# A recurrent block with a mixture of experts on one core: rows, halves of weights and the second layer's last tile in another order

## The reference, cut to what matters

```python
# x: (4, 256, 256) = 1024 tokens of 256 features
h = layernorm(x) * (1 + ca) + sa                    # sa .. gb: from silu(c) @ wmod, per batch
xn = rmsnorm(h, norm1_w)
left = gelu(xn @ left_W + left_b)
u = causal_depthwise_conv(xn @ right_W + right_b, conv_w, conv_b)     # 4 taps
right = rg_lru(u, ga_W, ga_b, gx_W, gx_b, a_param)  # two gates, then a scan over the tokens
x1 = left * right @ out_W + out_b + h
x1n = rmsnorm(x1, norm2_w)
mlp = gelu(x1n @ up1_W + up1_b) * (x1n @ up2_W + up2_b) @ down_W + down_b
x = x + ga * (mlp + x1)                             # "x2" in the kernel
h = layernorm(x) * (1 + cb) + sb
cw = top-2 of softmax(h @ gate_w), normalised       # 8 experts
moe = sum_e cw[:, e] * (gelu(h @ w1[e] + b1[e]) @ w2[e] + b2[e])
x = x + gb * (moe + h)
```

## Time and profile before

| what | value |
|---|---|
| median of 3 runs | 294.07 us (293.27 to 294.33) |
| the profiled execution's own time | 293.69 us |
| its span | 291.9 us |
| PE busy | 265.9 us (91%) |
| DVE busy | 200.3 us (69%) |
| ACT busy | 174.2 us (60%) |
| POOL busy | 128.9 us (44%) |

### The profile page before, as it was taken

One profiled execution on the slowest core, in us unless ns is written; L12 is line 12 of the kernel. 1 busy time (PEld: TensorE's weight loads), 2 busy tenths in 40 slices (PEclk: granted clock), 3 DMA queues, 4 the chain that ended last, 5 costly groups with the idle time before them and its releaser, 6 DMA issues.

```text
span 291.9 us, 4510 instructions
## 1 busy us (share of the span) xinstructions
PE 265.9 (91%) x1594; PEld 222.6 (76%) x1594; DVE 200.3 (69%) x459; ACT 174.2 (60%) x295; POOL 128.9 (44%) x104
## 2 busy tenths in 40 slices
PE   7997499999999999988999588999999999999970
PEld 2745246457788788866689588999999999999970
DVE  3659778937957777779877069685867676786520
ACT  4348449596089346960789139766859393939100
POOL 7009300000051312368075528738483839476651
PEclk9979599999999999999799869999999999999997
DMA  6990000000003757316145964929395766627233
GB/s 193 381 299 1 2 1 0 0 0 2 0 2 103 268 161 165 69 57 212 41 140 172 289 195 97 342 53 325 103 295 141 241 196 190 189 33 203 23 38 37
DMA packets 32838, 38.40 MB, mean 132 GB/s; under 512 B 7964, under 2 KB 28444, under 8 KB 32796
## 3 DMA queue, kind: packets, MB, share of 16 engines
q1 hardware_dynamic: 27184, 30.56, 33.4%
q0 software_dynamic: 4928, 7.44, 11.3%
q10 hardware_dynamic: 700, 0.07, 0.2%
HBM read 32.10 MB, written 8.90 MB: 140 GB/s over the span
## 4 chain that ended last, share of the span: by engine, by line
PE 50%; DVE 19%; DMA 9%; SPq 8%; issue 5%; ACT 4%; POOL 2%; POOLq 1%; DVEq 0%; ACTq 0%
PE bank L1007 15%; PE bank L1050 12%; PE bank L691 9%; SPq L505 5%; DVE u L1576 5%; PE bank L1044 3%; DMA x_rows<-blank 2%; PE bank L1043 2%; PE bank L891 2%; DMA gb_rows<-gb_table,meta 2%; DVE w_lo L1815 2%; DVE w_lo L1810 2%; SPq L509 1%; DMA x_tok<-in_L_attn_x 1%; PE bank L635 1%
## 5 line engine op out<-in xcount | busy, mean ns | idle before, releaser
L2109 POOL DMA_INDIRECT out_x<-y_tok,meta x24 | 53.3, 2219 | 38.2 <-DVE y_tok L1938 25.9
L1050 PE MATMUL bank<-w_hi,own 128*128 128x256 f32 x256 | 48.2, 283 | 0.0
L1920 DVE TENSOR_TENSOR own<-own_raw,own 128x256 fp32r<-128x256 f32 x64 | 27.2, 425 | 21.5 <-issue 13.2
L1007 PE MATMUL bank<-xe_hi,w_hi 128*128 128x320 f32 x128 | 39.9, 312 | 1.1 <-DVE xe_lo L1916 1.1
L1050 PEld LDWEIGHTS bank<-w_hi,own 128*128 128x128 f32 x256 | 40.9, 191 | 0.0
L1376 ACT ACTIVATE own_raw<-bank,b1c 128x320 f32<-128x320 f32 x64 | 33.5, 534 | 10.8 <-PE bank L1007 10.5
L1007 PE MATMUL bank<-xe_lo,w_hi 128*128 128x320 f32 x128 | 39.6, 309 | 0.0
L1007 PE MATMUL bank<-xe_hi,w_lo 128*128 128x320 f32 x128 | 39.6, 309 | 0.0
L1050 PE MATMUL bank<-w_lo,own 128*128 128x256 f32 x128 | 36.2, 283 | 0.0
L1382 ACT ACTIVATE own<-own_raw 128x320 fp32r<-128x320 f32 x64 | 29.8, 482 | 0.0
L2099 POOL DMA_INDIRECT gb_rows<-gb_table,meta x24 | 24.5, 1020 | 11.5 <-issue 6.7
(11 more groups left out here) (248 smaller groups left out, 636.5 us busy)
## 6 DMA issues: line engine op xcount, KB each, us to landing
e_raw<-in_L_ffn_w SPq DMA_DIRECT2D x16, 1024.0 KB
x_rows<-in_L_attn_x SPq DMA_DIRECT2D x1, 2560.0 KB
xe_tok<-x_rows SPq DMA_DIRECT2D x7, 256.0 KB
raw_m<-in_L_attn_up_W SPq DMA_DIRECT2D x2, 768.0 KB, 9.9
x_tok<-in_L_attn_x SPq DMA_DIRECT2D x2, 512.0 KB, 5.3
out_x<-x_tok SPq DMA_DIRECT2D x1, 1024.0 KB, 5.3
xe_tok<-x_rows SPq DMA_DIRECT2D x7, 128.0 KB
wmod<-in_L_wmod SPq DMA_DIRECT2D x1, 768.0 KB, 12.2
```

Of the source, the lines that this page charges most:

```text
L1007: ins = nc.tensor.matmul(bank[b][:, 0:CAP], l, r, start=(c == 0 and t == 0), stop=(c == KD - 1 and t == 2))
L1050: ins = nc.tensor.matmul(bank[b][0:n, 0:D], l, r, start=False, stop=(c == KE - 1 and t == 2))
L1920: nc.vector.tensor_tensor(own_lo[e % 2][:, f, :], own_raw[:, f % 4, 0:whole], own_hi[e % 2][:, f, 0:whole].bitcast(F32), ALU.subtract)
L2109: nc.gpsimd.indirect_dma_start(out_rows, bass.IndirectOffsetOnAxis(ap=ids[0:n, e, k, E:E + 1], axis=0), y_tok[e % 2][0:n, k, :], None, com ...
```

## The change

- **POOL** makes `wm_lo` as soon as its high halves are there; the split of the second bias comes after that and after the convolution (`conv_done`).
- **DVE, before the experts:** `rest(0)` goes from behind `v_of(KF + 5)`; two of the four picks of half 0 stand there, the other two behind the last `v_lo`. `w2_lo_of(0)` goes from behind `pick(1)` to behind `w1_lo_of(0)`, inside the MLP's last product. `rest(1)` goes too.
- **DVE, experts 0 and 1:** `rest(0)`, `rest(1)`, `rest(2)`, then `x_lo(1)` ahead of `keep_y(0, 0)`; `keep_y(0, 2)` and `w2_lo_of(1)` behind expert 1's low halves.
- **PE:** one gather ahead of `x2_and_logits(1, 1)`; the last tile of `second_layer(0)` behind `first_layer(1)`. The two banks of expert 0's gathers are exchanged.
- **ACT:** `w1_hi_of(2)` ahead of `x_hi(1)`, `keep_low(0)` behind `own_blocks(1)`.
- **SP:** the load of expert 2's first weights ahead of the wait for the `slot_a` scatters and `load_x(0)`.

```diff
-    take_at(("x0", 0), 3, 0)
-    take_at(("x0", 1), 1, 0)
+    take_at(("x0", 0), 1, 0)
+    take_at(("x0", 1), 3, 0)
...
                 load_w2(1)
+                sp.wait_ge(w1_lo_done, 2)
+                load_w1(2)
                 for t in range(TT):
                     sp.wait_ge(a_scattered[t], 16)
                 load_x(0)
-                sp.wait_ge(w1_lo_done, 2)
-                load_w1(2)
...
             down(1, [1], lambda: x2_and_logits(1, 0))
+            begin(("x0", 0))
+            gather(0, 0, 0)
             x2_and_logits(1, 1)
-            begin(("x0", 0))
-            for j in range(TH):
+            for j in range(1, TH):
                 gather(0, 0, j)
...
                 turn_of(1)
+                first_layer(1, EARLY, lambda: turn_of(2))
                 second_layer(0, [ST - 1])
-                first_layer(1, EARLY, lambda: turn_of(2))
...
                 w2_hi_of(1)
+                w1_hi_of(2)
                 x_hi(1)
+                own_blocks(1, lambda: x_hi(2))
                 act.wait_ge(rest_done, TT // 2)
                 keep_low(0)
-                w1_hi_of(2)
-                own_blocks(1, lambda: x_hi(2))
...
             v_of(KF + 5)
-            rest(0)
+            pick(0, range(TH // 2))
...
             nc.vector.tensor_tensor(v_lo[:, KF - 1, hs[1]], v_tile[(NH * KF - 1) % 4], v_hi[:, KF - 1, hs[1]].bitcast(F32), ALU.subtract).then_inc(v_lo_done, 1)
+            pick(0, range(TH // 2, TH))
             x2_of(1, [0])
             w1_lo_of(0)
-            pick(0)
-            rest(1)
+            w2_lo_of(0)
             x2_of(1, [1])
...
             pick(1)
-            w2_lo_of(0)
...
                     own_lo_of(0, f)
+                rest(0)
+                rest(1)
                 rest(2)
+                x_lo(1)
                 keep_y(0, 0)
                 rest(3)
                 keep_y(0, 1)
-                x_lo(1)
-                keep_y(0, 2)
-                w2_lo_of(1)
                 for f in range(KE):
...
                     own_lo_of(1, f)
+                keep_y(0, 2)
+                w2_lo_of(1)
...
+            for n in range(2):
+                pool.wait_ge(wm_hi_done, n + 1)
+                lo(wm_lo[:, n], raw_m[:, n], wm_hi[:, n], wm_lo_done)
+            pool.wait_ge(conv_done, NH * KH)
             pool.wait_ge(ffn_in, 16 * 4)
             pool.wait_ge(blank_done, 2)
...
             pool.wait_ge(b2_ready, 1)
-            for n in range(2):
-                pool.wait_ge(wm_hi_done, n + 1)
-                lo(wm_lo[:, n], raw_m[:, n], wm_hi[:, n], wm_lo_done)
-            pool.wait_ge(conv_done, NH * KH)
```

More of the change, by code:

```diff
@@ L1816, in w2_lo_of, with pick @@
                                         ALU.subtract).then_inc(w2_lo_done, 1)
-            def pick(hf):
+            def pick(hf, js=range(TH)):
                 if hf == 0:
@@ L1822, in pick @@
                     dve.wait_ge(gathered, 1)
-                for j in range(TH):
+                for j in js:
                     t = hf * TH + j
@@ L1979, in _ @@
                 nc.vector.memset(cwT[0:64, :], 0.0).then_inc(cw_cleared, 1)
-                rest(2)
-                rest(3)
+                for i in range(TT // 2):
+                    rest(i)
                 for i in range(TT // 2):
```

## The result

| | before | after |
|---|---|---|
| median, same chip, in turn | 294.20 us (293.27 to 294.83) | 282.79 us (281.83 to 283.80) |
| ratio, 95% interval | 1 | 0.9615 [0.957, 0.966] |
| profiled execution, its span | 293.69, 291.9 us | 283.80, 282.0 us |
| measured again, with the first experiments | 294.94 us | 283.04 us, 0.9565 [0.9491, 0.9638] |

The kernel is faster by 11.4 us (11.9 the second time); 280.4 was forecast, 13.3 less. The profiled execution, the slowest of its four, gained 9.9. Medians here are of all executions, and ratios leave out those over 1.5% above their kernel's fastest: one of `b_turn` (290.3 us, the profiled one) and two of `d_order` (289.17 us, and 339.78 us at a granted clock of 0.741).

The account below looks back on a forecast made before the run. PE, busy 91% of the span, was taken as the bound, each wait costing idle time and a lower clock. Gains of 5.0, 1.9 and 6.4 us sum to 13.3 off 293.69: 280.4 us, range 278 to 286.5.

Parts of the forecast that it names:

- POOL's order: First part, convolution of half 0 freed from POOL's subtraction: gates 3.8 plus clock 1.6 minus bias 0.4, 5.0 us gained.
- Gates: Behind the convolution of half 0: PE starts the gates at 29.05 instead of 32.89 us, 3.8 us gained.
- clock: First gate product on PE: without the long idle it takes 1.8 instead of 3.43 us, 1.6 us gained.
- bias: Recurrence of half 0 on DVE: POOL's bias split now meets it, delaying the out product, 0.4 us lost.
- The rival with 0.20: POOL's second subtraction gets in before the convolution's sixth operation; first part only 1.2 us, 284.2 us; chance 0.20.
- Around the last product: MLP's last product: picks of half 1, last gathers and expert 0 come 1.9 us earlier, bounds 0.7 and 2.9.
- The 0.89 us at `hT`: DVE's idle time at `hT`: transposes done in time with one gather less and the clock up, 0.9 us gained.
- the 1.3 us of the forecast for the scatters: Scatters ahead of expert 0: with `w2_lo` out of their way, the last one gains 1.3 us beyond the 1.9.
- Experts 0 to 2: Expert 0's full tiles to expert 2's start: waits and low clock 7.7, less 0.9 and 0.4, 6.4 us gained.
- the tokens 3.2 us earlier: they are there when PE arrives: Expert 1's tokens, asked for behind the weights: 3.2 us earlier, so PE's 2.9 us wait goes.
- expert 1's halves: PE's new wait from `turn_of(1)` to expert 1's first `x_lo`, through ACT and DVE: 0.9 us lost.
- The rival with 0.13: `gb_rows` land as late as before, past the harmless 165.7 us; last part 4.1, total 282.7 us; chance 0.13.

Follow-up runs that it names:

- b_turn: Changed kernel with expert 2's first weights (1 MB) asked for late and expert 1's transposes between expert 0's two full tiles; 287.20 us, ratio 0.9741.
- d_order: Changed kernel with ACT rounding the second up weights directly behind the first; profiled execution 287.7 us, others 283.82, 289.17 and 339.78 us.
- a_pool: Kernel before with POOL's reordering alone; 289.22 us, ratio 0.9805.
- a_trans: Kernel before with only the changes of PE, ACT, DVE and SP around experts 0 and 1; 293.51 us, ratio 0.9954.
- after_again: The changed kernel measured once more, in the same call as its parts; 283.04 us, ratio 0.9565.
- b_wlate: Changed kernel with expert 2's first weights (1 MB) asked for behind both experts' rows and rounded behind `x_hi(1)`; 286.43 us, ratio 0.9733.
- a_mid: Kernel before with only the changes around the MLP's last product (picks, second low half, gather, banks, residual additions); 290.62 us, ratio 0.9831.
- b_bias: Changed kernel with POOL's bias split directly behind the two low halves, ahead of the wait for the convolution; 281.15 us, ratio 0.9563.
- b_w2lo: Changed kernel with `w2_lo_of(0)` put back behind `pick(1)`; 285.13 us, ratio 0.9705.
- c_pause: Changed kernel with late megabyte, bias split moved, expert 0's gathers held, and last four scatters held until ACT has its gelu table; 281.58 us, ratio 0.9543.

## Why the prediction was right, and where its sum was off

- **POOL's order, 5.0 us: 5.2 measured.** Gates 4.4 instead of 3.8 (one subtraction takes 3.43 us here, not half of 7.60), clock 1.5 (1.6 forecast), bias 0.7 lost (0.4). The sixth operation of the convolution started at about 28.0, POOL's release came at 28.37 (ACT 26.88 + 1.49): DVE won by 0.4 us where 0.2 was forecast. The rival with 0.20 did not happen; `d_order` shows a lock of its kind, and a larger one. The slice at 29 to 36 us, which the forecast reads as 7, is a 5 in the earlier trace rows; no term hangs on it.
- **Around the last product, 1.9 us: 2.2 measured, half of it by luck.** The last `v_lo` came 0.86 us earlier against the last v (0.7 forecast). The 0.89 us at `hT` went with the full clock, and `a_pool` and `a_trans` lost them without any edit here: the term for them was a property of the one profiled execution, so the kernel's own gain is 1.1 us. Seven of eight scatters of half 1 take 0.96 to 1.16 us, one 2.01 beside the remaining low half: the 1.3 us of the forecast for the scatters are 1.15.
- **Experts 0 to 2, 6.4 us: 4.4 measured.** The step that failed is "the tokens 3.2 us earlier: they are there when PE arrives". Against the last v the last scatter did leave POOL 3.4 us earlier, but the tokens were asked for only 1.4 us earlier, since the megabyte asked for first delays the scatters' landing (4.3 instead of 2.3 us; 1.8 with the megabyte late). PE turned them 2.2 us later, against expert 0's first matmul, than it could have by the pace of before. It waited only 0.52 of these, because it was itself 1.65 us late: the gelus of expert 0 came late beside the denser scatters, a cost for which the sum had no term. The two are not two losses: with punctual gelus this execution would have waited for the tokens. In `after_again` PE did not wait for them and still turned them after 15.06 us, so there the gelus set the time; no run has both the early megabyte and the dense scatters with punctual gelus. From the turn on, the forecast is close: 1.0 us for expert 1's halves (0.9) and nothing lost to `gb_rows` (0.4).
- **`gb_rows`.** The rival with 0.13 did not happen: `keep_y(0, 0)` at 162.07 did not wait, well inside the 165.7. The early megabyte even seems to help: `meta` comes at 155 us, behind the gelus, where in `b_wlate` it came earlier and the gathers ran beside them.
- **The rest**, 110.3 us, is unchanged, as assumed. The fill of `x_rows` gave nothing back.
- **The start**, -1.9 us in both profiled executions of this kernel, is clock and no part of the change; without it the profiled execution would be near 281.9, 11.8 us less than before, of which 1.1 are the clock of the execution before.

## What to carry to other kernels

A large elementwise operation on POOL is placed by what DVE does beside it; with two of them in a row, one waiting operation of DVE came through between them and the next waited for the whole second: put them where DVE waits for PE. When a load is asked for earlier, look at which small transfers of other queues land in the same microseconds and who waits for those; the transfers that an instruction issues also come earlier, and may meet an engine that had the time for itself. A load asked for later is used later: look at what stands behind its first use. Parts of a change that prepare each other can't be costed alone: in the stretch from expert 0 to expert 2 the transition was worth 1.2 us by itself, the middle part 0.9, and all parts together 4.4. And before a gain is booked to an edit, compare the stretch with kernels that leave it alone: 1.1 of 2.2 us were the clock of one execution.

## What the runs showed that was not expected

- **ACT waits beside POOL's indirect transfers.** Gelus of expert 0 waited up to 2.0 us, with the releaser given as "remote", in every kernel in which `gb_rows` gathers ran beside them (`a_mid`, `b_wlate`, `b_turn`), and 0.8 us in `b_bias`, where none did. The first gelu was 1.2 us late (0.4 in `d_order`) in each kernel in which five of the eight scatters had been issued when ACT's step behind the table load began, and on time where it was four (before, `a_pool`, `a_trans`, `b_w2lo`, `c_pause`). What ACT waited for stays open: a packet of an instruction queue moved 0.5 to 0.6 us ahead of the late gelu in all eight profiles with the 1.2 us, but behind the first gelu in `d_order`, `b_w2lo` and `c_pause`.
- **A scatter's landing beside a 1 MB load** took 4.1 to 4.9 us from the last issue to the next load on SP instead of 2.1 to 2.3, and 1.7 to 3.4 where the load came later. `a_mid`, whose load fell beside the last two scatters, had 5.5.
- **Eight warm-up matmuls at either clock**, 1.91 or 3.60 us, with about the same 0.7 to 1.1 us of waiting ahead of them, moved whole executions by 1.9 us.
